# First feed-forward of a two-layer decoder on one core: transposes of the next x before the down product, weights fetched during the scan

## The reference

```python
def ternarize_weight(w):
    abs_mean = jnp.maximum(jnp.mean(jnp.abs(w)), 1e-05)
    thr = 0.7 * abs_mean
    q = jnp.where(w > thr, one, jnp.where(w < -thr, -one, 0))
    return w + stop_gradient(q * abs_mean - w)
h = einsum('bsd,hd->bsh', x, ternarize_weight(w_fc))      # w_fc 1280 x 512
h = square(relu(h))
return einsum('bsh,dh->bsd', h, ternarize_weight(w_proj)) # w_proj 512 x 1280
...
x = layernorm(x + L0_attn(x)); x = layernorm(x + L0_xattn(ctx, x))
x = layernorm(x + L0_ffn(x, w_fc, w_proj))
```

## Time and profile before

| | before |
|---|---|
| median of 3 runs | 3131.87 us (3131.31 to 3134.49) |
| the profiled execution, time | 3131.36 us |
| the profiled execution, span | 3129.7 us |
| PE busy | 2780.9 us (89%) |
| DVE busy | 2044.2 us (65%) |
| ACT busy | 1103.4 us (35%) |
| POOL busy | 692.4 us (22%) |

### The profile page before, as it was taken

The page is one execution under the profiler, slowest core; times in us unless marked ns, Lnnn a source line. Parts: engine busy times, 40 slices in busy tenths (PEclk is TensorE's granted clock), DMA queues, the critical chain, the costliest instruction groups (busy, mean ns, idle before and its releaser), DMA issues.

```text
span 3129.7 us, 29594 instructions
## 1 busy us (share of the span) xinstructions
PE 2780.9 (89%) x8882; PEld 1509.6 (48%) x8882; DVE 2044.2 (65%) x3924; ACT 1103.4 (35%) x2014; POOL 692.4 (22%) x569
## 2 busy tenths in 40 slices
PE   6787888788775878789999999999999999899998
PEld 2323323333334664345554555445554555378886
DVE  3996996996996444658882788457873878233222
ACT  4334334325222311125551455235541555211111
POOL 1552552553540014541110111011101111000000
PEclk9898898988887889999999999999999999999999
DMA  3231331221331111310002000110012000500000
GB/s 113 94 114 41 107 102 52 97 101 58 104 134 48 47 62 52 141 42 14 17 18 81 24 14 18 49 59 18 14 29 76 18 18 18 177 27 28 28 14 14
DMA packets 76608, 178.67 MB, mean 57 GB/s; under 512 B 9139, under 2 KB 25779, under 8 KB 75446
## 3 DMA queue, kind: packets, MB, share of 16 engines
q1 hardware_dynamic: 65526, 139.71, 13.7%
q0 software_dynamic: 5472, 21.01, 1.8%
q10 hardware_dynamic: 5472, 16.32, 1.5%
HBM read 147.32 MB, written 29.69 MB: 57 GB/s over the span
## 4 chain that ended last, share of the span: by engine, by line
PE 55%; DVE 23%; issue 8%; DMA 5%; POOL 4%; ACT 3%; SPq 1%; DVEq 0%; POOLq 0%; ACTq 0%
PE bank L475 31%; PE bank L761 7%; DVE h L1159 5%; DMA Cb<-bc_dram 3%; PE bank L716 3%; PE bank L775 3%; PE bank L776 2%; PE bank L779 2%; POOL h L1468 2%; DVE sm L1392 2%; DVE h L1164 2%; DVE p L1403 1%; DVE val L1331 1%; PE bank L804 1%; PE bank L805 1%
## 5 line engine op out<-in xcount | busy, mean ns | idle before, releaser
L1468 POOL TENSOR_TENSOR h<-du,Bb 128x1024 f32<-128x1024 f32 x128 | 345.9, 2722 | 262.2 <-DMA Cb<-bc_dram 253.8
L886 ACT ACTIVATE bank<-dt,A 128x512 f32<-128x512 f32 x256 | 176.8, 691 | 438.6 <-DVE h L1159 438.5
L1159 DVE TENSOR_TENSOR_SCAN h<-bank,h 128x512 f32<-128x512 f32 x256 | 297.9, 1204 | 17.6 <-POOL h L1468 17.4
L597 PE MATMUL bank<-h,ident 128*128 128x512 f32 x256 | 162.2, 719 | 127.7 <-DVE h L1164 127.5
L1008 ACT ACTIVATE p<-bank,sm,rq 128x512 f32<-128x512 f32 x256 | 198.9, 777 | 208.6 <-DVE sm L1396 208.6
L191 POOL TENSOR_SCALAR rstd<-mv 128x1 f32<-128x1 f32 x96 | 33.2, 346 | 947.3 <-DVE mv L185 947.3
L1523 POOL TENSOR_TENSOR rq<-rq,mhalf 128x4 f32<-128x4 f32 x64 | 65.5, 1024 | 791.1 <-DVE rq L1383 791.1
L475 PE MATMUL bank<-pT,v 128*128 128x512 f32 x512 | 233.1, 598 | 3.1 <-ACT pT L831 3.1
L1164 DVE TENSOR_TENSOR h<-h,Cb 128x1024 f32<-128x1024 f32 x128 | 229.7, 1795 | 8.8
L475 PE MATMUL bank<-xT,wxq 128*128 128x512 f32 x512 | 230.6, 593 | 3.2 <-ACT xT L831 3.2
L761 PE MATMUL bank<-woh,oT 128*128 128x512 f32 x512 | 223.8, 598 | 9.5 <-DMA woh<-in_Wo 7.5
(11 more groups left out here) (199 smaller groups left out, 5222.9 us busy)
## 6 DMA issues: line engine op xcount, KB each, us to landing
Bb<-bc_dram SPq DMA_DIRECT2D x64, 512.0 KB, 3.5
Cb<-bc_dram SPq DMA_DIRECT2D x64, 512.0 KB, 4.8
x_dram<-xo POOLq DMA_DIRECT2D x16, 1024.0 KB, 4.7
xc<-x_dram SPq DMA_DIRECT2D x16, 1024.0 KB, 5.2
woh<-in_Wo SPq DMA_DIRECT2D x64, 256.0 KB, 2.7
idx<-in_idx SPq DMA_DIRECT2D x64, 129.0 KB, 2.1
w_dram<-val SPq DMA_DIRECT2D x64, 129.0 KB, 2.5
xc<-in_x SPq DMA_DIRECT2D x4, 1024.0 KB, 7.9
```

Source lines behind the costliest of these rows:

```text
L597: pe.matmul(bank[4 + e][:, :], ident[:, :], h[:, U % HR, 0, :], start=(q == 0), stop=False)
L886: act.activation(bank[6 + n][:, :], dt[:, et, :], ACT.Exp, scale=A[:, et, 2 * q + n:2 * q + n + 1]).then_inc(dA_ready, 1)
L1159: dve.tensor_tensor_scan(h[:, s, n, :], bank[6 + n][:, :], h[:, s, n, :], 0.0, ALU.mult, ALU.add).then_inc(scanned, 1)
L1468: pool.tensor_tensor(h[:, U % HR, :, :], du[:, et:et + 1, :].to_broadcast([P, 2, S]), Bb[:, w % 2, :, :], ALU.mult).then_inc(dBu_ready, 1)
```

## The change

- SyncE issues both weights, behind the scan's transfers. w_fc goes as soon as the last chunk's attention projections are done (a semaphore of its own, fc_loaded), w_proj after the four sums of the last chunk's first norm. The wait for all of stage 0's stores is gone; each load of x waits for its own chunk.
- ACT sums |w_fc| and |w_proj|, one behind the other. DVE sums neither.
- TensorE transposes the first chunk before the ones matmul. In each chunk the order is up product, transposes of the next chunk, down product. The first tile of the down product waits for each hidden slice by itself, and the first up product waits for q1 alone.
- DVE makes x_lo of the first chunk between mask and ternary weight of w_fc, and that of chunk c + 1 before the norm of chunk c. ACT rounds the next x behind the last hidden slice.
- tneg lies behind x_lo in memory. The loops over chunk pairs are written out for TensorE, ACT and DVE.

```diff
@@ memory @@
-        tneg = Space(nc, s2.at)("tneg", [P, KD * F0])
         wabs = Space(nc, s2.at)("wabs", [P, KD * F0])
         hr = s2("hr", [P, 2, S]); h2 = s2("h2", [P, 2, S])
         x_hi = s2("x_hi", [P, KD, S], F32R); x_lo = s2("x_lo", [P, KD, S], F32R)
+        tneg = Space(nc, s2.at)("tneg", [P, KD * F0])
@@ SyncE @@
-                sp.wait_ge(stored, STORED0 + 16 * B)
-                simple_stage(1, rows_of)
+                sp.wait_ge(a_full, START + A0[0] + after(B - 1, PER_A[0], 24))
+                sp.dma_start(w1[:], io["w_fc"].rearrange("(k p) n -> p k n", p=P)).then_inc(fc_loaded, 16)
+                sp.wait_ge(ln_sum, START + after(B, 8, -4))
+                weights(1, w2, io["w_proj"])
+                for c in range(B):
+                    load_chunk(1, c, c % 2, rows_of)
@@ TensorE @@
+                def down1(c):
+                    for t in range(NT):
+                        pe.wait_ge(ln_sum, START + T0[1] + after(c, 4, t + 1 - 4))
+                        for f in range(KF0):
+                            if t == 0:
+                                pe.wait_ge(h_ready, START + after(c, KF0, f + 1))
+                            pe.matmul(bank[4 + t][:, :], h_hi[:, f, t * P:(t + 1) * P], q2[:, f, :], start=(f == 0), stop=False)
+                            m = pe.matmul(bank[4 + t][:, :], h_lo[:, f, t * P:(t + 1) * P], q2[:, f, :], start=False, stop=(f == KF0 - 1))
+                        m.then_inc(v_full, 1)
+                pe.wait_ge(ln_sum, START + T0[1])
+                turn1(0)
                 pe.wait_ge(abs_sum, START + 2)
                 group(bank[6][:, 0:2], [(ones[:, :], am[:, 0, 0:2])], abs_all)
-                pe.wait_ge(tern, START + 2)
...
+                pe.wait_ge(tern, START + 1)
+                for c in range(B):
+                    inner(c)
+                    if c + 1 < B:
+                        turn1(c + 1)
+                    if c == 0:
+                        pe.wait_ge(tern, START + 2)
+                    down1(c)
@@ ACT @@
-                act.wait_ge(ln_sum, START + after(B, 8, -4))
-                for dst, name in ((w1, "w_fc"), (w2, "w_proj")):
-                    act.dma_start(dst[:], io[name].rearrange("(k p) n -> p k n", p=P)).then_inc(stage_loaded[1], 16)
...
+                act.wait_ge(fc_loaded, START + 16)
+                act.activation(wabs[:, :], w1[:, :, :].rearrange("p k n -> p (k n)"), ACT.Abs, accum_out=am[:, 0, 0:1])\
+                    .then_inc(abs_sum, 1)
...
+                        if c + 1 < B:
+                            x_rounded(c + 1)
@@ DVE @@
-                dve.tensor_reduce(am[:, 0, 0:1], w1[:, :, :].rearrange("p k n -> p (k n)"), AX.X, ALU.add,
-                                  apply_absolute_value=True).then_inc(abs_sum, 1)
...
                     dve.wait_ge(tern_n, START + n + 1)
+                    if n == 0:
+                        x_rest(0)
...
                         rest(KF0 - 1)
+                        if c + 1 < B:
+                            x_rest(c + 1)
                         dve.wait_ge(stored, STORED0 + 16 * B + 16 * c)
                         norms(1, c, ...)
```

More of the change, by code:

```diff
@@ L270, in build @@
         x_hi = s2("x_hi", [P, KD, S], F32R); x_lo = s2("x_lo", [P, KD, S], F32R)
+        tneg = Space(nc, s2.at)("tneg", [P, KD * F0])
         s2h = Space(nc, shared_end)
         h_hi = s2h("h_hi", [P, KF0, S], F32R); h_lo = s2h("h_lo", [P, KF0, S], F32R)
-        abs_sum = sem("abs_sum"); abs_all = sem("abs_all"); thr_set = sem("thr_set")
+        fc_loaded = sem("fc_loaded"); abs_sum = sem("abs_sum"); abs_all = sem("abs_all"); thr_set = sem("thr_set")
         tern_n = sem("tern_n"); tern = sem("tern")
@@ L608, in _, with turn1, inner @@
             if stages >= 2:
+                def turn1(c):
+                    turn(1, c, 0, xc[:, c % 2], x_loaded[c % 2], x_count(1, c // 2))
+                def inner(c):
+                    pe.wait_ge(x_split, START + after(c, KD, KD))
+                    for f in range(KF0):
+                        d = a_bank(1, c, 4 + f)
+                        group(d[:, :], [(q1[:, k, f * P:(f + 1) * P], x[:, k, :]) for k in range(KD) for x in (x_hi, x_lo)], a_full)
+                def down1(c):
+                    for t in range(NT):
+                        pe.wait_ge(ln_sum, START + T0[1] + after(c, 4, t + 1 - 4))
+                        for f in range(KF0):
+                            if t == 0:
[3 more added lines that the diff above has]
+                        m.then_inc(v_full, 1)
@@ L904, in _, with x_rounded @@
             if stages >= 2:
-                act.wait_ge(ln_sum, START + after(B, 8, -4))
-                for dst, name in ((w1, "w_fc"), (w2, "w_proj")):
-                    act.dma_start(dst[:], io[name].rearrange("(k p) n -> p k n", p=P)).then_inc(stage_loaded[1], 16)
-                act.wait_ge(stage_loaded[1], START + L0[1])
                 act.wait_ge(y_added, START + after(B, NU, 0))
+                act.wait_ge(fc_loaded, START + 16)
+                act.activation(wabs[:, :], w1[:, :, :].rearrange("p k n -> p (k n)"), ACT.Abs, accum_out=am[:, 0, 0:1])\
+                    .then_inc(abs_sum, 1)
+                act.wait_ge(abs_sum, START + 1)
+                act.wait_ge(stage_loaded[1], START + 16)
                 act.activation(wabs[:, :], w2[:, :, :].rearrange("p k n -> p (k n)"), ACT.Abs, accum_out=am[:, 0, 1:2])\
                     .then_inc(abs_sum, 1)
[L914 to L919, removed]
+                def x_rounded(c):
+                    for k in range(KD):
+                        d = filled(1, c, k)
+                        bring(x_hi[:, k, :], d[:, :])
+                act.wait_ge(abs_sum, START + 2)
+                x_rounded(0)
+                for c in range(B):
+                    for p in (c % 2,):
                         def rounded(f):
@@ L1211, in _, with x_rest @@
             if stages >= 2:
-                dve.wait_ge(stage_loaded[1], START + L0[1])
-                dve.tensor_reduce(am[:, 0, 0:1], w1[:, :, :].rearrange("p k n -> p (k n)"), AX.X, ALU.add,
-                                  apply_absolute_value=True).then_inc(abs_sum, 1)
+                def x_rest(c):
+                    for k in range(KD):
+                        dve.wait_ge(a_done, START + A0[1] + after(c, PER_A[1], k + 1))
+                        dve.tensor_tensor(x_lo[:, k, :], bank[k][:, :], x_hi[:, k, :], ALU.subtract).then_inc(x_split, 1)
                 dve.wait_ge(abs_all, START + 1)
```

## The result

The changed kernel took 3081.24 us (median of 4 runs, 3079.03 to 3085.63) against 3133.18 us (3131.31 to 3134.92): a ratio of 0.9836, 95% interval 0.9824 to 0.9848, or 52 us less. The forecast was 3080.8 (3076 to 3090). The profiled execution has a span of 3079.0 us and took 3081.09.

What follows compares the result with a forecast made beforehand. TensorE was the engine to fill, held up by the start, gaps around down products and slow clock spells. 16.0 + 18.4 + 3.8 + 7.5 + 5.4 = 51.1 us off 3131.87 gives 3080.8 us, range 3076 to 3090.

Steps and rivals of the forecast that it cites:

- start, to the first up product: Start of the first feed-forward: early loads, sums on ACT and reordered DVE work begin the first up product 16.0 us earlier.
- gaps behind three down products: Between a down product and the next up product: transposes, rounding and split moved ahead, so 18.37 us of gaps vanish.
- gaps before down products: Between up and down product: 2.67 us gaps for three chunks, none for the last, gaining 3.8 us of 11.81.
- clock, up products 1 to 3: TensorE stays at the fast clock level, so up products 1 to 3 take 18.7 us each, gaining 7.5 us.
- clock, down products: TensorE stays at the fast clock level, so the four down products take 18.3 us each, gaining 5.4 us.
- first up product: First up product's length: DVE's mask and q2 delaying its first square was put at cost 0.
- Rival 1: TensorE's clock dips on: 3085.6 us with one dip per chunk, 3093.7 with all of them; chance 0.12.
- Rival 2: Early w_fc load delays the scan's Cb by up to 4.8 us or arrives late: 3085.6 or 3088.3 us; chance 0.07.
- Rival 3: DVE and ACT pace the up products, 3.3 us lost in each of three: 3090.7 us; chance 0.04.
- Rival 4: Denser stream drives TensorE to the slow clock for good, 88 us slower if all matmuls ran so: 3220; chance 0.01.

Runs made afterwards that it cites:

- start_only: Changed kernel with the old chunk order taken back, keeping only the new start of the stage; stage 215.9 us, time 3114.5 us, ratio 0.9939 to before.
- order_only: Kernel before with only the new chunk order, loads, sums and thresholds as before; profiled twice, stage 197.4 us both times, time 3106.3 and 3103.1 us.
- written_out: Kernel before with only stage 1's loops over chunk pairs written out; stage 232.4 us, time 3133.3 us, ratio 1.0001.
- filled: Kernel before, loops written out, with unused matmuls added in TensorE's gaps; profiled twice, stage 220.3 and 220.4 us, time 3126.7 and 3127.7 us.
- halves: Changed kernel with the ones matmul ahead of chunk 0's transposes and w_fc ternarized in two halves; stage 178.9 us, time 3082.1 us.
- all_ten: Changed kernel with one wait for all ten hidden slices ahead of each down product; stage 187.6 us, time 3091.0 us.
- late_weights: Changed kernel with ACT issuing both weight loads where the kernel before did; stage 186.0 us, time 3092.8 us.

## Why the prediction was right, term by term

Terms as forecast, and as the two first profiles have them:

| term | forecast | measured | from |
|---|---|---|---|
| start, to the first up product | 16.0 | 16.7 | (969.62 - 929.23) - (948.94 - 925.25) |
| gaps behind three down products | 18.4 | 18.4 | none is left |
| gaps before down products | 3.8 | 3.4 | 11.8 - 3 x 2.80 |
| clock, up products 1 to 3 | 7.5 | 7.6 | 63.6 - 56.0 |
| clock, down products | 5.4 | 6.0 | 78.6 - 72.6 |
| first up product | 0 | -1.3 | 20.31 to 21.60 |
| sum | 51.1 | 50.8 | |

The pieces of a chain are cut where one hands over to the next, and the records of back-to-back blocks overlap by 0.16 us or more. By the records alone, from a block's first start to its last end, the two clock terms are 7.1 and 5.0 us, and the gap terms are larger by the difference. DVE's sum over w_fc stood in the chain of before ahead of the rows:

```profile
940.12 5.49 DVE am L1213
```

- The start: the sums ended 2 us ahead of the transposes as forecast, and the four steps on DVE had their durations of before. By the durations in the two chains the 16.7 us are three things, and what else differs adds up to nothing: the sum over w_fc on DVE (5.5), which is gone; q2's mask and ternary work (2.90 + 5.56 = 8.5 us), which moved behind the start of the first up product; and the tail of the last layer norm (from 937.45 to 940.12, 2.7 us), for which the transposes no longer wait. The prediction worked out the new start as one chain and did not price these parts. The sum moved off DVE and the early fetch cost 4.9 and 3.9 us when each was taken back alone from the finished kernel; these needn't add up.
- The gaps before the down products: TensorE stood still 0.87 us for the last ReLU, where the sum had 0.70.
- The first up product was 1.3 us longer, which the sum had at nothing. DVE's delay is not the reason: TensorE was busy 21.56 of the 21.60 us. The slow spell was longer, 13 matmuls at the slow spacing where the kernel before had 7 (14 in start_only, 7 in order_only, one in written_out).
- The clock was the one term that rested on a behaviour. `filled` shows that the pauses made it (11.5 us came back with TensorE kept busy in them), both profiles of `order_only` and of the changed kernel show that a pause of 0.9 us followed by 16 transposes does not bring it back: in twelve of twelve such places the down product behind took 18.4 us, by its records, and the next up product 18.7; in halves a pause of 1.55 us before the first transposes did not either. Rival 1 did not come true. The Trainium skill, TensorE: Matmul & The Clock Gate, section A second HAM failure mode: psum-queue depth-cycling, has the clock swing with short idle moments of TensorE between groups of matmuls: pauses of 0.9 us with transposes behind them did not do that here, one of 2.9 us did (all_ten).
- Rival 2: w_fc landed 11.2 us after its issue, and Cb, issued 0.6 us ahead of it, 5.43 us after (4.8 in the median of all 64). The last Cb took 5.4 to 5.6 us in all six profiles with the early load and 4.6 to 4.9 in the eight without, so the load did delay it, by some 0.7 us and not 4.8; no later end of the scan shows (late_weights). Rival 3: with DVE busy 13.29 of 18.6 us the up products still took 18.68. Rival 4 did not occur.
- The 52 us against 50.7 of the stage, and the forecast that hit within 1 us, are partly luck: the spans around the stage moved by -4.0 (stage 0) and +4.0 us (behind it) between the two profiles, for no edit that was found to reach them, and cancelled. Within the stage the first up product's -1.3 and the gaps' -0.4 were met by +0.7 of the start and +0.7 of the clock.

## What to carry to other kernels

Where the engine that sets the pace waits for a chain that the next chunk needs (load, transposes, split), issue that chain ahead of the last long block of this chunk, not behind it. Price a pause of TensorE with what follows it: here 30 us of pauses cost some 12 us more in matmuls at the slow level. When single executions scatter by more than an edit is worth, measure the edited stage in the profile between two fixed instructions, and the whole time over many runs.

## What the runs showed of the hardware

- The clock's fall can come with a delay and does not depend on the pause alone: after the same pause of 2.9 to 3.0 us the down product of chunk 2 stayed fast in all four profiles with the old order and no filler (18.4 us), those of chunks 1 and 3 took 20 us in all four, and that of chunk 0 took 20 us in three and 18.4 in start_only. In the first profile they fell after some 1.2 and 1.0 us of fast matmuls, that of chunk 0 at once.
- A slow spell can also move elsewhere. The qkv product of the next stage, whose code is the same in all kernels, took 173.8 to 174.3 us from its first to its last matmul in ten profiles, and 175.8 to 176.2 in all four of filled and order_only. One line on that product, from start_only and from filled (ns min/median/max, first and last start):

```profile
L479 PE MATMUL bank<-wqkv,xT x256: 486/486/585, 1160.3 to 1334.1; 128*128 128x384 f32 x128
```

```profile
L476 PE MATMUL bank<-wqkv,xT x256: 486/486/1004, 1160.3 to 1336.5; 128*128 128x384 f32 x128
```

The median is the same and the longest is 1004 ns in place of 585. In the 5 us from 1160 on the granted clock was 0.50 in filled and 8 of these matmuls were done, in start_only it was 1.00 and 15 were done; in the 40 us from there the same 64 matmuls keep TensorE busy 23.27 against 20.90 us. The 2.4 us are a slow spell at the product's start. So a later stage can give back 2 us of what another won. When it starts is not what decides: both kernels here begin it at 1160.3. What does was not settled, nor where the other 2 us between filled's stage and its time went.
